# Attention scores in two layouts, softmax sums from a block of ones, and an unrolled attention stage

## The reference

```python
hid = silu(einsum('bnf,if->bni', x_cat, W_h) + b_h)          # x_cat: 16 values and 16 ones
h = einsum('bni,hi->bnh', hid, W_o) + b_o + einsum('bnf,hf->bnh', x_cat, W_r) + b_r   # (32, 64, 256)
z = layernorm(h).reshape(b, s, 16, 16)                        # 16 heads of 16
q, k, v = z @ Wq.T, z @ Wk.T, z @ Wv.T
attn = softmax(einsum('bqhd,bkhd->bhqk', q, k) / sqrt(256), axis=-1)
h = h + einsum('bhqk,bkhd->bqhd', attn, v).reshape(b, s, e) @ W_out.T + b_out
h = h + real(ifft(fft(layernorm(h)) @ w)) + bias
```

## Time and profile before

| | us |
|---|---|
| median of 3 runs | 179.96 |
| lowest and highest | 178.42 and 181.06 |
| span of the profiled execution | 178.8 |

### The profile page before, as it was taken

The page is one execution under the profiler, slowest core; times in us unless marked ns, Lnnn a source line. Parts: engine busy times, 40 slices in busy tenths (PEclk is TensorE's granted clock), DMA queues, the critical chain, the costliest instruction groups (busy, mean ns, idle before and its releaser), DMA issues.

```text
span 178.8 us, 5271 instructions
## 1 busy us (share of the span) xinstructions
PE 137.4 (77%) x1770; PEld 114.3 (64%) x1770; DVE 133.8 (75%) x379; ACT 117.8 (66%) x292; POOL 78.2 (44%) x132
## 2 busy tenths in 40 slices
PE   0299979898888896787959759695696878857672
PEld 0299979897756685575747547584584766744541
DVE  0668474866597799877998986889899896999240
ACT  3494757677898697683868766596686783856200
POOL 4018942462043469625245354343624535254120
PEclk9999999999999999969999996999999988999667
DMA  4680000000000000000000000000000000010001
GB/s 52 173 261 7 4 0 0 2 0 0 2 0 4 0 22 17 29 0 31 0 29 29 0 29 7 22 29 0 29 3 26 29 0 29 0 33 29 4 4 55
DMA packets 7290, 4.44 MB, mean 25 GB/s; under 512 B 3312, under 2 KB 7024, under 8 KB 7280
## 3 DMA queue, kind: packets, MB, share of 16 engines
q1 hardware_dynamic: 6992, 4.21, 8.1%
q10 hardware_dynamic: 288, 0.10, 0.2%
HBM read 2.20 MB, written 2.10 MB: 24 GB/s over the span
## 4 chain that ended last, share of the span: by engine, by line
PE 50%; DVE 36%; issue 6%; ACT 3%; DMA 2%; DVEq 1%; ACTq 0%
PE bank L917 10%; PE bank L906 10%; DVE sums L707 6%; DVE xh L715 6%; PE bank L816 6%; PE bank L896 5%; DVE xblk L659 5%; PE bank L820 4%; PE bank L879 4%; DVE stats L697 4%; DVE h L695 4%; DVE hid_lo L592 3%; PE bank L926 3%; PE bank L884 2%; DMA xs<-in_x 2%
## 5 line engine op out<-in xcount | busy, mean ns | idle before, releaser
L488 POOL TENSOR_TENSOR half_sums<-probs 128x256 f32<-128x256 f32 x32 | 23.2, 726 | 51.5 <-ACT probs L319 51.5
L879 PE MATMUL bank<-ident,xh 128*128 128x128 f32 x32 | 6.8, 294 | 25.6 <-DVE xh L715 25.6
L666 DVE TENSOR_REDUCE rowmax<-bank 128x4 f32<-128x256 f32 x64 | 24.9, 409 | 1.7 <-PE bank L866 1.7
L319 ACT ACTIVATE probs<-probs 128x256 f32<-128x256 f32 x64 | 24.6, 417 | 2.0 <-DVE probs L671 2.0
L671 DVE TENSOR_TENSOR probs<-bank,rowmax 128x256 f32<-128x256 f32 x64 | 24.9, 409 | 0.0
L592 DVE TENSOR_TENSOR hid_lo<-hidT,hid_hi 128x512 fp32r<-128x512 f32 x16 | 15.4, 964 | 10.1 <-ACT hidT L284 10.0
L879 PEld LDWEIGHTS bank<-ident,xh 128*128 128x128 f32 x32 | 3.2, 141 | 29.6 <-issue 27.7
L917 PE MATMUL bank<-value_w,onT 128*128 128x256 f32 x64 | 20.3, 447 | 0.6 <-DVE onT L680 0.6
L906 PE MATMUL bank<-mix_w,sideT 128*128 128x256 f32 x64 | 20.0, 442 | 0.6 <-ACT sideT L323 0.5
L312 ACT ACTIVATE inv_rows<-inv_sum 128x128 f32<-128x128 f32 x32 | 8.1, 300 | 16.4 <-DVE inv_sum L711 16.4
L342 ACT ACTIVATE pT<-bank 128x512 f32<-128x512 f32 x32 | 17.5, 597 | 1.4 <-PE bank L938 0.7
(11 more groups left out here) (118 smaller groups left out, 332.9 us busy)
## 6 DMA issues: line engine op xcount, KB each, us to landing
out<-y SPq DMA_DIRECT2D x16, 128.0 KB, 1.7
wo_raw<-in_W_o SPq DMA_DIRECT2D x1, 512.0 KB, 3.9
wout_raw<-in_W_out SPq DMA_DIRECT2D x1, 256.0 KB, 3.1
fr<-in_wr SPq DMA_DIRECT2D x1, 256.0 KB, 4.5
fi<-in_wi SPq DMA_DIRECT2D x1, 256.0 KB, 4.5
xs<-in_x SPq DMA_DIRECT2D x1, 128.0 KB, 3.4
bout_bc<-in_b_out SPq DMA_DIRECT2D x1, 128.0 KB, 4.2
cosine_sb<-in_cosine SPq DMA_DIRECT2D x1, 128.0 KB, 4.4
```

The costliest lines, as they stand in the source:

```text
L319: nc.scalar.activation(probs[:, j, :], probs[:, j, :], ACT.Exp).then_inc(exp_done, 1)
L488: nc.gpsimd.tensor_tensor(half_sums[:, quads, :, :].rearrange("p q h k -> p (q h) k"), pr[:, :, 0, :], pr[:, :, 1, :], ALU.add).then_inc(h ...
L666: nc.vector.tensor_reduce(rowmax[:, j, :], bank[j][:, 0:D].rearrange("p (h k) -> p h k", k=TOK), AX_X, ALU.max).then_inc(max_done, 1)
L879: last = pe.transpose(bank[SIDE_BANK][:, half * P:(half + 1) * P], xh2[:, half * P:(half + 1) * P], ident[:])
```

## The change

- `scores` stays as it was for the maximum, with two buffers for `xzT` and `qT`. `shift`, `turn_p`, `copy_p`, `halve_sums` and `inverse_sums` go.
- The maxima are written at spread columns of `rowmax` (two for each quad in each half), two transposes (`turn_max`) put them on rows, ACT copies them to `maxT`. `keyed_scores` makes the scores a second time in the other half of the same four banks, with keys on partitions, and `take_max` adds minus the maximum by a product with the constant `minus_rows`. ACT takes the exponential out of PSUM straight into `pT`.
- `weigh` multiplies `pT` also by the constant `pair_ones`, which gives the sums on the same rows as the values. DVE's `divide` transposes them in 32x32 blocks, inverts one column in 16, spreads that by a second block transpose and scales.
- `residual_bias` is made for one tile at a time on POOL in the second stage, into two buffers, in place of four tiles at a time.
- `norm2(i-1)` stands on DVE in the next step, behind the first maximum; `place_crossed` moves ahead of `residual`.
- All steps of the second stage are written out in place of loops; the stage's matrices are made before `scores(0)`, each pair in one bank and copied at once.
- Two more constants are loaded.

The diff, cut to its core. Removed lines are left out where the code above has them.

```diff
+    minus_rows = np.where(r[:, None] % 32 == r[None, :] // TOK, -1.0, 0.0).astype(np.float32)
+    pair_ones = (r[:, None] // TOK == np.arange(32)[None, :] // HD).astype(np.float32)
...
+        VALUE_BANK, HALFWAY_BANK, MIXW_BANK = 2, 3, 7
+        X_BANK, PV_BANK, MAX_BANK, PROJ_BANK = 4, 5, 6, 7
+        FREQ_BANK, SIDE_BANK = MAX_BANK, PROJ_BANK
...
+            sp.dma_start(minus_rows[:], a["minus_rows"]).then_inc(att_loaded, 16)
+            sp.dma_start(pair_ones[:], a["pair_ones"]).then_inc(att_loaded, 16)
...
+            def copy_max(t):
+                act.wait_ge(max_turned, t + 1)
+                nc.scalar.activation(maxT[:], bank[MAX_BANK][:, 0:D], ACT.Copy).then_inc(max_copied, 1)
+            def exponent(t):
+                for j in range(QUADS):
+                    act.wait_ge(keyed_done, QUADS * t + j + 1)
+                    nc.scalar.activation(pT[:, j, :], bank[j][:, D:2 * D], ACT.Exp).then_inc(exp_done, 1)
...
+            def step(i):
+                if i + 2 < T:
                     copy_xT(i + 2)
+                if i + 1 < T:
+                    copy_max(i + 1)
+                if i >= 1:
+                    copy_side(i - 1)
+                if i + 1 < T:
+                    exponent(i + 1)
+                if i + 2 < T:
                     copy_q(i + 2)
+                if i + 3 < T:
+                    normalize(i + 3)
+            act.wait_ge(att_loaded, 112)
+            normalize(0)
             silu(T - 1, 1)
             copy_xT(0)
+            copy_halfway()
             copy_h(T - 2, 0)
+            copy_value_weights()
+            normalize(1)
             copy_q(0)
+            copy_mix_weights()
+            copy_h(T - 1, 1)
             nc.scalar.activation(warm[:], half_neg[:, 0:1], ACT.Exp)
             copy_xT(1)
             copy_q(1)
+            normalize(2)
+            copy_max(0)
+            exponent(0)
+            for i in range(T + 1):
+                step(i)
...
+            def residual_bias(t):
+                if t >= 2:
+                    pool.wait_ge(h2_done, t - 1)
+                pool.wait_ge(h_copied, t + 1)
+                nc.gpsimd.tensor_tensor(hb[t % 2][:], h_all[:, t, :], bout_bc[:], ALU.add).then_inc(hb_done, 1)
...
+            def step(i):
+                if i + 2 < T:
+                    place_same(i + 2)
+                if i + 1 < T:
+                    residual_bias(i + 1)
+                inv_std2(i)
+                add_bias(i)
+            inv_std1(0)
             place_same(0)
+            residual_bias(0)
+            place_same(1)
             inv_std1(1)
+            for i in range(T):
+                step(i)
...
+                nc.vector.tensor_reduce(rowmax[:, :, 32 * j:32 * j + 2],
+                                        bank[j][:, 0:D].rearrange("p (a e k) -> p a e k", e=2, k=TOK),
                                         AX_X, ALU.max).then_inc(max_done, 1)
...
             def divide(t):
                 dve.wait_ge(pv_done, t + 1)
+                nc.vector.transpose(sumsT[:], bank[PV_BANK][:, D:2 * D]).then_inc(sums_turned, 1)
+                dve.wait_ge(sums_turned, t + 1)
+                nc.vector.reciprocal(inv_sum[:], sumsT[:].rearrange("p (c e d) -> p c e d", e=2, d=HD)[:, :, :, 0]
+                                     ).then_inc(inv_done, 1)
+                dve.wait_ge(inv_done, t + 1)
+                nc.vector.transpose(inv_rows[:].rearrange("p (c e d) -> p (c e) d", e=2, d=HD),
+                                    inv_sum[:].rearrange("p c e -> p (c e)").unsqueeze(2).to_broadcast([P, D // HD, HD])
+                                    ).then_inc(inv_spread, 1)
+                dve.wait_ge(inv_spread, t + 1)
                 nc.vector.tensor_tensor(onT[:].rearrange("p a t -> p (a t)"), bank[PV_BANK][:, 0:D],
...
+            def step(i):
+                if i + 1 < T:
+                    maximum(i + 1, 0)
+                if i >= 1:
+                    norm2(i - 1)
+                if i + 1 < T:
+                    for j in range(1, QUADS):
+                        maximum(i + 1, j)
+                if i < T:
+                    divide(i)
+                if i + 2 < T:
+                    place_crossed(i + 2)
+                if i < T:
                     residual(i)
...
+            def keyed_scores(t):
                 for half in range(HALF):
                     for b in range(2):
                         for j in range(QUADS):
+                            if half == 0 and b == 0:
+                                pe.wait_ge(max_done, QUADS * t + j + 1)
+                            rows32 = slice(32 * j, 32 * j + 32)
+                            at0 = D + half * P + TOK * b
+                            pe.matmul(bank[j][:, at0:at0 + TOK],
+                                      xzT[t % 2][rows32, 2 * half + b, :, :].rearrange("p e k -> p (e k)"),
+                                      qT[t % 2][rows32, half, TOK * b:TOK * b + TOK],
+                                      start=(half == 0 and b == 0), stop=False, skip_group_check=True)
+            def take_max(t):
+                pe.wait_ge(max_copied, t + 1)
+                for j in range(QUADS):
+                    rows32 = slice(32 * j, 32 * j + 32)
+                    pe.matmul(bank[j][:, D:2 * D], minus_rows[rows32, :], maxT[rows32, :],
+                              start=False, stop=True, skip_group_check=True).then_inc(keyed_done, 1)
+            def turn_max(t):
+                pe.wait_ge(max_done, QUADS * (t + 1))
+                if t == 0:
+                    pe.wait_ge(h_copied, T)
+                if t >= 1:
+                    pe.wait_ge(max_copied, t)
+                if t >= 3:
+                    pe.wait_ge(y_set, t - 2)
+                for half in range(HALF):
+                    last = pe.transpose(bank[MAX_BANK][:, half * P:(half + 1) * P], rowmax[:, half, :], ident[:])
+                last.then_inc(max_turned, 1)
...
+            def weigh(t):
+                pe.wait_ge(exp_done, QUADS * (t + 1))
+                pe.wait_ge(xblk_same, t + 1)
+                pe.wait_ge(xblk_crossed, t + 1)
+                if t >= 1:
+                    pe.wait_ge(on_set, t)
+                for j in range(QUADS):
+                    pe.matmul(bank[PV_BANK][32 * j:32 * j + 32, D:2 * D], pair_ones[:], pT[:, j, :], start=True, stop=True)
+                for half in range(HALF):
+                    for b in range(2):
+                        cols = slice(half * P + TOK * b, half * P + TOK * (b + 1))
+                        for j in range(QUADS):
+                            last = pe.matmul(bank[PV_BANK][32 * j:32 * j + 32, cols],
+                                             xblk[t % 2][:, b, half * P + 32 * j:half * P + 32 * j + 32],
+                                             pT[:, j, cols], start=True, stop=True)
                 last.then_inc(pv_done, 1)
...
+            def step(i):
+                if i + 1 < T:
                     scores(i + 1)
+                if i + 2 < T:
+                    turn_x(i + 2)
+                if i < T:
+                    weigh(i)
+                if i + 1 < T:
+                    turn_max(i + 1)
+                if i >= 1:
+                    turn_side(i - 1)
+                if i + 1 < T:
+                    keyed_scores(i + 1)
+                    take_max(i + 1)
+                if i + 2 < T:
+                    query(i + 2)
+                if i < T:
                     project(i)
+                if i >= 1:
+                    mix_freq(i - 1)
             hidden(T - 1, 1)
+            for c in range(2):
+                rows_spectrum(c)
+            turn_x(0)
             mix(T - 2, 0)
+            value_weights()
             query(0)
+            for c in range(HALF):
+                cols_spectrum(c)
             mix(T - 1, 1)
+            turn_x(1)
             pe.wait_ge(silu_done, T)
+            pe.wait_ge(value_copied, 1)
             scores(0)
             query(1)
+            turn_max(0)
+            keyed_scores(0)
+            take_max(0)
+            for i in range(T + 1):
+                step(i)
 # ---- launch: one core; inputs and outputs as the reference has them ----
```

451 lines of the change are left out of this document (113 added, 338 removed).

## The result

The changed kernel takes 186.93 us (median of 4 runs, 185.35 to 187.5), the one before beside it 179.54 us (178.42 to 181.06). The ratio is 1.042, with a 95% interval of 1.034 to 1.050: slower by about 4%. The profiled span grew from 178.8 to 185.7 us.

The account below looks back on a forecast made before the run. No engine full; a chain of handovers, mainly DVE and PE, bounds each attention step. Residual(0) at 60.3 plus 110.6 gives 170.9; with 7.7 a 178.6 span; plus 1.2 gives 179.8, rounded to 180 us; range 173.5 to 187.5.

Parts of the forecast that it names:

- the likeliest case: Whole kernel: no clock falls between first and last tile, 7.4 to 7.65 us per step, 180 us; chance 0.41.
- a dear keyed_scores: Attention step on PE: load and product in turn, 1.28 us, 6.7 us more in all, 186.7; chance 0.14.
- The passage: Between first stage and attention loop: more PE work and the exp table load put residual(0) at 60.3, from 59.11.
- clock falls as before: Rival for the whole kernel: same chain with three lower-clock stretches, 4.3 us more, 184.3; chance 0.20.
- The period: Attention step, from one end of norm2 (L715) to the next: 7.52 us against 7.17 before.
- The disputed term: PE's second scores in each attention step: eight rounds of a 128-column load, 0.86 us, with products alongside.
- the lower bound by L896: Second scores as cheap as the value products' row, 0.43 us: 6.9 less in all, 173; chance with milder form 0.21.
- The other loop has room: Attention steps: exp(i+1) before scores(i+2) is not binding; last exp near N+4.7, PE free at N+5.3.
- The falls of the clock in the loop: Attention loop: three earlier dips, 4.3 us, most likely gone because PE idles less, 1.2 us per step.
- the fetch of code: Written-out steps: some 15 more instruction packets, each stopping PE 1 us, would give 195; chance 0.04.
- the collisions: First stage: three clashes of DVE's hid_lo remainder with POOL's hb_all go, gaining 2.7 us.
- The tail: After residual(15), to the end of the kernel: unchanged at 7.7 us.

Follow-up runs that it names:

- the filled passage: Changed kernel with value weights and spectra behind scores(0) on PE, tile 0's maxima and the exp table load earlier: 181.32 us, ratio 1.013.
- the useless products: Changed kernel with seven extra 128x256 products on PE in the waits before the attention loop, into a bank nobody reads yet: 185.31 us, ratio 1.027.
- query behind project: Changed kernel with query(i+2) issued after project(i) instead of ahead of it: 180.05 us, ratio 0.997.
- narrow loads: Changed kernel with 64 stationary columns instead of 128 in keyed_scores, half of the keyed scores left out: 180.03 us, ratio 1.005.

## Why the prediction was right and wrong

The time, 186.93, is inside the range (173.5 to 187.5), but near its upper end, and the likeliest case was "no change" (180, its own range 177.5 to 183). That end was put there for a dear keyed_scores, which did not come about; that the time still fell inside is luck. The sum was 178.6 for the span; it is 185.7. The 7.1 us by the sum's own terms (the last three rows add up to it):

| term | forecast | measured | difference |
|---|---|---|---|
| last mix ends | 47.9 | 47.81 | -0.1 |
| query(1) starts | 50.6 | 50.90 | +0.3 |
| residual(0) | 60.3 | 64.14 | +3.8 |
| residual(0) to residual(15) | 110.6 | 112.87 | +2.3 |
| residual(15) to the end | 7.7 | 8.7 | +1.0 |

**The passage** is where the forecast failed. Up to query(1) it held within 0.3 us. The step that failed is the next one: from there every product was priced by rows at full clock, though the working itself had PE idle from the end of scores(0) to query(1), and the rival "clock falls as before" named an idle stretch of 1.9 us just there. It was priced by the dips of the loop (4.3 us in all), not as a dip at that place. Its cost, 4.0 us, is shown by the filled passage (9.20 for 13.24), and by the useless products (some 3.8). At full clock the stretch from query(1) to residual(0) is shorter than the 9.7 forecast, which hid 0.5 of the 4.0. The cost itself varies: with query behind project and with narrow loads, whose code for the passage is the same up to there and which wait as long, the dip lasted 6.8 us instead of 10.2. That PE's waiting ahead of it is the cause is shown so far as filling the wait removes the dip in both kernels; splitting it in two (0.70 and 1.38) does not.

**The period** was right in its mechanism and mis-sized by 0.15 of 7.52. With N the end of norm2 at 112.91: turn_max N+1.05 (forecast 1.14), keyed_scores N+1.64 (1.70), take_max N+2.58 (2.56), query N+3.18 (3.09), project N+3.73 (3.53), residual N+4.89 (4.76), next N at N+7.67 (7.52). The disputed term, keyed_scores, was taken as 0.86 by the load of 128 columns; it is 0.94, and the narrow loads show that the larger part goes with the loaded columns. It is far from the lower bound by L896 (0.43) and from the rival's 1.28. The largest miss is query, 0.55 until project where 0.44 was taken: four products of 128 columns, with a switch of tiling ahead of them. One step in the middle took 8.02, in every variant of the changed kernel 0.36 longer than its neighbours and always the eleventh. Up to project its rows stand where they stand in the other steps; only the residual starts 0.36 later, though nothing that it needs is late. What holds it stays open. Times 15, and the odd step, make 2.3.

**"The other loop has room"** held for the changed kernel: query behind project shortened the step at once. How little room it is shows where project was moved ahead, which had been expected to bring 1.1 us and brought 0.10. PE's busy time per step was put at 6.2 of 7.5, 83%; it is 6.60 of 7.67, 86%.

**The falls of the clock in the loop** are gone, as was leaned to, and their 4.3 us too, and with them the fourth one, in the last step, which the forecast had named but not counted. That it is the shorter pause of PE is consistent with it: the waits are 1.06 now; with the old attention unrolled they are 1.62 and nothing falls either; with 2.08 the dips are there. But the earlier trace rows has a dip behind 1.79 and the useless products one behind 1.72, while the filled passage has none behind the very same wait of 1.72, so no length of the pause decides by itself. The gain of the unrolling is shown by the kernel before unrolled; the forecast had costed it at nothing but the fetch of code. The fetch stopped nothing that the profile shows: 18 packets of instructions came, where some 21 were counted, and it names no wait for them. Whether the odd 0.36 of the eleventh step is one is not known.

**The first stage** gave back what the collisions had cost: the last mix was forecast at 47.9 and ended at 47.81. The collisions cost 2.8 us, where 2.7 had been counted. That the mark was met within 0.1 is partly luck, though: in the variants that leave this part of the code as it is the last mix ends between 46.58 and 48.02.

**The tail** was taken over as it was, 7.7. The clock falls once more at 180.5, and the last mix_freq runs at half speed:

```profile
180.74 2.08 PE L853 MATMUL bank<-mix_w,sideT 128*128 128x256 f32 x4 [0.47 <-ACT sideT L342]
```

It takes 2.08 where the same four products take 1.03 in the loop: the 1.0 us.

**Of the rivals** none came true as a whole: the total is that of "keyed_scores dearer" (186.7), by another mechanism, since keyed_scores took 0.94 and not 1.28. With the 4.0 us of clock in the passage the forecast's own sum would have been a span of 182.6, or 183.8 as a time.

## What to carry to other kernels

A pause of TensorE is to be priced twice, once for itself and once for the clock behind it: 2.2 us of waiting at the passage between two stages cost up to 4.0 us more in work done at half speed, and moving work there that had to be done anyway took back both, 6.3 us. Where two in-order engines hand over in turn, look for all loops of about the same length before pricing one; an edit to one gives little where another is just behind (project ahead: 0.10 of the 1.1 expected), while an edit to a piece of both gives its whole length (norm2: 0.41 of 0.41). A GpSimd sum that is not urgent is best held back by a wait until VectorE's instruction on the critical way is through; here that one line was worth 0.41 of the 7.67 us of a step.

## What the runs showed of the hardware

- A 32x32-block transpose of 128x256 float32 on DVE takes 0.43 from PSUM and 0.45 from SBUF, near the 0.41 of a maximum over the same size, and was never late.
- Thirty-two loads of 32 rows, four row groups abreast: 0.94 us with 128 columns, 0.62 with 64, products of 64 columns in both. The time falls with the columns, but does not halve. The Trainium skill (TensorE: Matmul & The Clock Gate, section LDWEIGHTS) says that a load of 32 rows takes as long as one of 128, since the columns matter; the 0.94 agrees with that (8 x 0.107 = 0.86), not the bound of 0.43.
- With nothing changed but the loops written out, a step went from 7.17 to 6.95 us, and the three dips of the clock between 70 and 150 us did not occur in the profiled run (mean clock 0.993; 0.952 to 0.981 in the three others); with each step 0.46 us longer and PE's wait at 2.08 instead of 1.62 they were back.
- A dip of the clock that began in the passage lasted 10.2 us in five kernels, 6.8 in two others; single dips inside the loop of the old attention lasted 3.4.
- Behind the same wait of 1.72 us at the same instruction the clock fell in one run (useless products) and stayed in another (filled passage).
- The same code of the first stage took 1.77 us per tile in some executions and 1.82 in others, 0.6 us over twelve tiles.
